# Macaron block with a mixture of experts: the two experts of a token found by MAX8 and FIND_INDEX8 instructions instead of pairwise comparison

## What is computed

```python
logits = xf @ gate_w                                  # (tokens, 8)
top_logits, top_idx = jax.lax.top_k(logits, 2)
top_gates = jax.nn.softmax(top_logits, axis=-1)
gates = jnp.sum(jax.nn.one_hot(top_idx, 8) * top_gates[..., None], axis=1)
h = gelu(jnp.einsum('nd,edh->neh', xf, w1) + b1)      # 8 experts, hidden 256
out_e = jnp.einsum('neh,ehd->ned', h, w2) + b2
routed = jnp.einsum('ne,ned->nd', gates, out_e)
shared = gelu(xf @ shared_w1 + shared_b1) @ shared_w2 + shared_b2
x = x + 0.5 * (routed + shared)
```

## The kernel before

| group | rank begins | TensorE stages after logits, with their plan start | place ready | place begins |
|---|---|---|---|---|
| 0 | 65.2 | hidden 65.1, acc 68.8 | 70.1 | 73.2 |
| 1 | 343.6 | hidden 342.9, hidden 346.7 | 348.5 | 350.4 |
| 2 | 780.5 | hidden 779.1, hidden 782.9 | 785.4 | 786.6 |
| 3 | 1141.0 | hidden 1140.9, hidden 1144.7 | 1145.9 | 1148.4 |

## Time and profile before

### The profile page before, as it was taken

How to read it: one execution, slowest core, us unless ns; L and a number is a source line. 1 busy time by engine, 2 the same in 40 slices (tenths; PEclk the granted TensorE clock), 3 DMA queues, 4 the chain that set the end, 5 groups by cost and what they waited for, 6 DMA issues and landing times.

```text
span 1339.3 us, 10709 instructions
## 1 busy us (share of the span) xinstructions
PE 1047.6 (78%) x3296; PEld 574.9 (43%) x3296; DVE 731.5 (55%) x1130; ACT 593.6 (44%) x1008; POOL 439.6 (33%) x429
## 2 busy tenths in 40 slices
PE   5998888982978878968938287867977698969884
PEld 3545555332534444444313142344444443536552
DVE  3311000067879898979999885978988520200000
ACT  3423433233425888557323333357666541314332
POOL 4153443202553353331000246032452212154442
PEclk8998999995989989979968587989988899779887
DMA  8954554424144675773344624265685425034544
GB/s 284 332 171 87 94 95 79 79 58 134 36 98 109 173 143 117 160 196 93 94 111 87 206 56 93 60 179 112 134 215 108 68 37 112 32 64 95 94 85 56
DMA packets 60204, 155.15 MB, mean 116 GB/s; under 512 B 10578, under 2 KB 10578, under 8 KB 57974
## 3 DMA queue, kind: packets, MB, share of 16 engines
q0 software_dynamic: 29568, 60.90, 26.9%
q1 hardware_dynamic: 30582, 93.58, 22.6%
HBM read 99.74 MB, written 58.88 MB: 118 GB/s over the span
## 4 chain that ended last, share of the span: by engine, by line
DMA 33%; PE 27%; DVE 12%; POOL 10%; ACT 8%; issue 8%; SPq 1%; POOLq 0%; ACTq 0%; DVEq 0%
DMA x_rows<-ys,into_i 14%; DMA out_rows<-ys,into_i 10%; PE misc L867 6%; POOL slots L1538 6%; PE hps L736 5%; DMA xs<-x_normal,rows_i 4%; PE yps L805 3%; PE hps L789 3%; PE yps L748 2%; PE xps L719 2%; DVE run L1355 2%; ACT ys L975 2%; DMA xin<-in_x 1%; DMA xin<-x_rows 1%; ACT xin L996 1%
## 5 line engine op out<-in xcount | busy, mean ns | idle before, releaser
L805 PE MATMUL yps<-w_all,hidden_sb 128*128 x368 | 209.5, 700 | 55.8 <-ACT hidden_sb L962 55.0
L789 PE MATMUL hps<-w_all,hidden_sb 128*128 x736 | 188.2, 403 | 8.5 <-ACT hidden_sb L945 8.5
L1355 DVE TENSOR_TENSOR_SCAN run<-pwx,trig 128x512 f32<-128x512 f32 x128 | 149.5, 1210 | 46.0 <-ACT trig L1046 45.2
L789 PEld LDWEIGHTS hps<-w_all,hidden_sb 128*128 128x128 f32 x736 | 148.3, 207 | 54.3 <-issue 36.3
L1550 POOL DMA_INDIRECT xs<-x_normal,rows_i x92 | 106.1, 1153 | 139.2 <-PE xps L780 119.9
L975 ACT ACTIVATE ys<-yps,slots 128x512 f32<-128x512 f32 x92 | 63.1, 686 | 169.8 <-PE yps L805 62.3
L1563 POOL DMA_INDIRECT out_rows<-ys,into_i x46 | 77.5, 1685 | 166.5 <-ACT ys L975 94.2
L805 PEld LDWEIGHTS yps<-w_all,hidden_sb 128*128 128x128 f32 x368 | 74.3, 214 | 131.8 <-issue 129.8
L736 PE MATMUL hps<-xnT,sw_sb 128*128 128x512 f32 x256 | 129.9, 662 | 0.8 <-ACT xnT L919 0.8
L1563 POOL DMA_INDIRECT x_rows<-ys,into_i x46 | 77.8, 1691 | 153.9 <-DMA x_rows<-ys,into_i 85.0
L748 PE MATMUL yps<-sw_sb,hidden_sb 128*128 128x512 f32 x256 | 124.0, 629 | 0.0
(11 more groups left out here) (199 smaller groups left out, 1587.4 us busy)
## 6 DMA issues: line engine op xcount, KB each, us to landing
qx<-q_cols SPq DMA_DIRECT2D x128, 256.0 KB
x_normal<-xin SPq DMA_DIRECT2D x32, 256.0 KB
w_all<-in_w_experts SPq DMA_DIRECT2D x8, 1024.0 KB, 8.3
xin<-x_rows SPq DMA_DIRECT2D x32, 256.0 KB, 4.7
turns_sb<-in_w_out SPq DMA_DIRECT2D x3, 1536.0 KB
xin<-in_x SPq DMA_DIRECT2D x16, 256.0 KB, 3.8
x_rows<-ys POOLq DMA_DIRECT2D x16, 256.0 KB
q_cols<-xin SPq DMA_DIRECT2D x16, 256.0 KB
```

Source lines behind the costliest of these rows:

```text
L789: t = PE.matmul(hps[:, bank, 0:H], xT[:, j % 2, c, :], w_all[:, bass.ds(expert[j] + c * H, H)], start=c == 0, stop=c == KC - 1)
L805: t = PE.matmul(yps[:, bank, :], hb[:, j % 2, ec, :], w_all[:, bass.ds(expert[j] + (KC * H + ec * D), D)], start=ec == 0, stop=ec == EC - 1)
L1355: t = VE.tensor_tensor_scan(run[:, c, :], pwx[:, n // M, :], trig[:, n % 2, c, :], 0.0, ALU.mult, ALU.add)
```

## The change

`rank_logits` is rewritten. Four `max` instructions, one for each tile of 128 tokens, read eight logits from PSUM and write them sorted (`most`), four `max_index` instructions read them again with the sorted values and write their places (`most_at`, uint32). `diff` is the difference of the first two sorted values; `sel` is a comparison of the first two places with the constants 0 to 7 (`expert_no`, a new iota on POOL in place of the two memsets of `two`); `chosen` is the sum of the two halves of `sel`. `lg`, `rank`, `lr` and `two` are gone. `chosen` is now the last of the five signalled steps (item 4), `diff` is item 2, and the PSUM bank of the logits is free after the last `max_index` (item 1). The planner's cost of `rank` goes from 4.8 to 3.0.

```diff
-            piece("DVE", ("rank", q), 4.8, ("PE", ("logits", q)), ...)
+            piece("DVE", ("rank", q), 3.0, ("PE", ("logits", q)), ...)
...
             elif s[0] == "logits":
-                xps_uses.append((s, ranking.at((s[1], 0))))
+                xps_uses.append((s, ranking.at((s[1], 1))))
...
-                pe.wait_ge(*ranking.at((GB * g + 1, 6)))
+                pe.wait_ge(*ranking.at((GB * g + 1, 4)))
...
-                act.wait_ge(*ranking.at((q, 10)))
+                act.wait_ge(*ranking.at((q, 2)))
...
-                VE.tensor_copy(lg[:, :, :], xps[:, bank, 0:TB * E].rearrange("p (t e) -> p t e", e=E)
-                               ).then_inc(*ranking.of((q, 0)))
+                for tb in range(TB):
+                    t = VE.max(most[:, tb, :], xps[:, bank, tb * E:(tb + 1) * E])
+                t.then_inc(*ranking.of((q, 0)))
                 vec.wait_ge(*ranking.at((q, 0)))
-                VE.tensor_tensor(cmp_b[:, :, :, :], other, own, ALU.is_equal).then_inc(*ranking.of((q, 1)))
-                VE.tensor_tensor(cmp_a[:, :, :, :], other, own, ALU.is_gt).then_inc(*ranking.of((q, 2)))
+                for tb in range(TB):
+                    t = VE.max_index(most_at[:, tb, :], most[:, tb, :], xps[:, bank, tb * E:(tb + 1) * E])
+                t.then_inc(*ranking.of((q, 1)))
+                if q > 0:
+                    vec.wait_ge(*gate_exp.at(q - 1))
+                VE.tensor_tensor(diff[:, :], most[:, :, 1], most[:, :, 0], ALU.subtract).then_inc(*ranking.of((q, 2)))
                 vec.wait_ge(*ranking.at((q, 1)))
-                VE.tensor_tensor(cmp_b[:, :, :, :], cmp_b[:, :, :, :], low, ALU.mult).then_inc(*ranking.of((q, 3)))
+                VE.tensor_tensor(sel[:, ts, :, :], most_at[:, :, 0:2, None].broadcast_to([P, TB, 2, E]),
+                                 expert_no[:, None, None, :].broadcast_to([P, TB, 2, E]),
+                                 ALU.is_equal).then_inc(*ranking.of((q, 3)))
                 vec.wait_ge(*ranking.at((q, 3)))
...
-                VE.tensor_scalar(chosen[:, ts, :], rank[:, :, :], 1.5, None, ALU.is_lt).then_inc(*ranking.of((q, 6)))
...
+                VE.tensor_tensor(chosen[:, ts, :], sel[:, ts, 0, :], sel[:, ts, 1, :],
+                                 ALU.add).then_inc(*ranking.of((q, 4)))
```

More of the change, by code:

```diff
@@ L150, in macaron @@
         block_of = sb("block_of", [P, NB])
-        two = sb("two", [P, 2])
         minus_half = sb("minus_half", [P, TB])
@@ L161, in macaron @@
         rstd_a = sb("rstd_attn", [P, 3, TB])
-        lg = sb("lg", [P, TB, E])
+        most = sb("most", [P, TB, E])
+        most_at = sb("most_at", [P, TB, E], mybir.dt.uint32)
+        expert_no = sb("expert_no", [P, E])
         cmp_a = sb("cmp_a", [P, TB, E, E])
         cmp_b = sb("cmp_b", [P, TB, E, E])
-        rank = sb("rank", [P, TB, E])
         sel = sb("sel", [P, GT, 2, E])
@@ L169, in macaron @@
         pair = sb("pair", [P, GT, 2, E])
-        lr = sb("lr", [P, TB, 2])
         diff = sb("diff", [P, TB])
@@ L310, in plan_job @@
             piece("PE", ("logits", q), 6.0, *kept_rows, *start[:1], bank=[("xps", ("DVE", ("rank", q)))])
-            piece("DVE", ("rank", q), 4.8, ("PE", ("logits", q)), *start[2:], *([("DVE", ("gates", q - 1))] if q else []),
+            piece("DVE", ("rank", q), 3.0, ("PE", ("logits", q)), *start[2:], *([("DVE", ("gates", q - 1))] if q else []),
                   *([("DVE", ("place", g - 1))] if g and not second else []))
@@ L586, in macaron @@
         stats_made = signal("s_stats", [(q, i) for q in staged("load", "DVE") for i in range(2)])
-        ranking = signal("s_ranking", [(q, i) for q in staged("rank", "DVE") for i in range(11)])
+        ranking = signal("s_ranking", [(q, i) for q in staged("rank", "DVE") for i in range(5)])
         gating = signal("s_gating", [(q, i) for q in staged("gates", "DVE") for i in (0, 1, 2, 7, 3, 4, 5, 6)])
@@ L1120, in rank_logits @@
                 ts = slice(q % GB * TB, (q % GB + 1) * TB)
-                other = lg[:, :, None, :].broadcast_to([P, TB, E, E])
-                own = lg[:, :, :, None].broadcast_to([P, TB, E, E])
-                low = before[:, None, :, :].broadcast_to([P, TB, E, E])
                 vec.wait_ge(*consts.at(16))
                 vec.wait_ge(*logits_made.at(q))
-                VE.tensor_copy(lg[:, :, :], xps[:, bank, 0:TB * E].rearrange("p (t e) -> p t e", e=E)
-                               ).then_inc(*ranking.of((q, 0)))
+                for tb in range(TB):
+                    t = VE.max(most[:, tb, :], xps[:, bank, tb * E:(tb + 1) * E])
@@ L1133, in rank_logits @@
                 vec.wait_ge(*ranking.at((q, 3)))
-                VE.tensor_tensor(cmp_a[:, :, :, :], cmp_a[:, :, :, :], cmp_b[:, :, :, :],
-                                 ALU.add).then_inc(*ranking.of((q, 4)))
-                vec.wait_ge(*ranking.at((q, 4)))
-                VE.tensor_reduce(rank[:, :, :], cmp_a[:, :, :, :], AX.X, ALU.add).then_inc(*ranking.of((q, 5)))
-                vec.wait_ge(*ranking.at((q, 5)))
                 if q >= GB:
                     vec.wait_ge(*counted.at(q // GB - 1))
-                VE.tensor_scalar(chosen[:, ts, :], rank[:, :, :], 1.5, None, ALU.is_lt).then_inc(*ranking.of((q, 6)))
@@ L1142, in rank_logits @@
-                VE.tensor_tensor(sel[:, ts, :, :], rank[:, :, None, :].broadcast_to([P, TB, 2, E]),
-                                 two[:, None, :, None].broadcast_to([P, TB, 2, E]),
-                                 ALU.is_equal).then_inc(*ranking.of((q, 7)))
-                vec.wait_ge(*ranking.at((q, 7)))
-                VE.tensor_tensor(pair[:, 0:TB, :, :], sel[:, ts, :, :], lg[:, :, None, :].broadcast_to([P, TB, 2, E]),
-                                 ALU.mult).then_inc(*ranking.of((q, 8)))
@@ L1148, in rank_logits @@
-                vec.wait_ge(*ranking.at((q, 8)))
-                VE.tensor_reduce(lr[:, :, :], pair[:, 0:TB, :, :], AX.X, ALU.add).then_inc(*ranking.of((q, 9)))
-                vec.wait_ge(*ranking.at((q, 9)))
-                if q > 0:
-                    vec.wait_ge(*gate_exp.at(q - 1))
-                VE.tensor_tensor(diff[:, :], lr[:, :, 1], lr[:, :, 0], ALU.subtract).then_inc(*ranking.of((q, 10)))
+                VE.tensor_tensor(chosen[:, ts, :], sel[:, ts, 0, :], sel[:, ts, 1, :],
+                                 ALU.add).then_inc(*ranking.of((q, 4)))
@@ L1587, in tables @@
                 GE.memset(gcols[:, :, 2 * (E + 1):BR], 0.0)
-                GE.memset(two[:, 0:1], 0.0)
-                GE.memset(two[:, 1:2], 1.0)
                 GE.memset(no_rows[:, :, 1], 0.0)
@@ L1594, in tables @@
                 GE.iota(steps_of[:, :], pattern=[[P, E]], base=0, channel_multiplier=0,
+                        allow_small_or_imprecise_dtypes=True)
+                GE.iota(expert_no[:, :], pattern=[[1, E]], base=0, channel_multiplier=0,
                         allow_small_or_imprecise_dtypes=True)
```

## The result

| | before | after |
|---|---|---|
| median | 1333.6 us of four runs (1325.69 to 1348.18) | 1299.18 us of four runs (1298.54 to 1300.38) |
| span of the profiled execution | 1339.3 us | 1297.3 us |
| TensorE, VectorE, ScalarE, POOL busy | 1047.6, 731.5, 593.6, 439.6 us | 1018.4, 718.9, 586.2, 447.5 us |
| mean granted TensorE clock | 0.878 | 0.894 |

The ratio on record is 0.9714, with a 95% interval of 0.9674 to 0.9755, so the kernel is some 38 us faster.

A forecast was written before the change was run, and what follows sets the result against it. No single engine was taken to bound the kernel. Group 3's 3.4 us passed whole and half of the others' 10.8 us made 8.8 us off the profiled 1340.6 us; against the median, 1330 us, range 1314 to 1350.

The forecast's parts named there:

- The new ranking, 1.8 us: Each rank on VectorE: 1.8 us against 3.28, with 12 instructions for the sorted values and their places.
- The bank, nothing: Logits' PSUM bank is free 1.3 us after the rank begins, before at 0.2; costed at nothing, at worst 1.1 us.
- Job 4's rank, 1.5 us: In the attention stretches, where VectorE is nearly full, job 4's shorter rank gives 1.5 us.
- Group 3, 3.4 us whole: At the kernel's end the counting comes before the second `hidden` stage: 3.4 us less, passed on whole.
- Group 0, 1.9 of 3.9 us: Counting moves ahead of `acc`, 3.9 us earlier; the first block also waits for TensorE, so only 1.9 us gained.
- Group 1, a toss, 3.4 us: Counting ready exactly when the second `hidden` is; taken as moved ahead of it, 3.4 us less, a coin's toss.
- Group 2, 4.0 us: Counting stays, but `gates` goes before the gelu and VectorE's `place`, so the scatter begins 4.0 us earlier.
- The rival of an order that falls well: Shared-expert stages leave the way of the last attention batch's rows: 1318 us, with like luck before it 1310; chance 0.1.
- The two rivals by order: TensorE's order near the last attention batch turns against the kernel, 1350 us, chance 0.2, or falls well, 1310 us, chance 0.1.

The follow-up runs named there:

- the hand-made swap: New ranking, planner's cost 4.8, group 3's counting and job 7's exponential moved ahead of job 7's hidden and gelu; against the kernel before: 1335.36 us, 0.9993.
- the one that I tried: Attention sines moved ahead of block copies in ScalarE's order; ratios to the kernel before: 1.0054 in that kernel, 0.9989 in the new ranking with cost 1.6.

## Why the prediction was wrong

**The new ranking, 1.8 us.** Right, and a little dear: 1.57 us. The four MAX8 took 0.39 us together, a pitch of 0.08; the pairs came every 0.14 us, as two instructions, by the larger count that was taken. At a lone instruction's price for each it would have been 2.8 us; that didn't hold, for no wait stands inside the two fours and their instructions overlap in the rows: the FIND_INDEX8 that starts at 55.61 lasts to 55.78, and the next MATCH_VALUE_LOAD starts at 55.69. (The Trainium skill, "VectorE: DVE Perf Modes", section "The TRN2 errata", which the prediction set beside this end, speaks of instructions that read SBUF. MAX8 and FIND_INDEX8 read PSUM here, so these rows don't test it on them.) (That finding the index is a pair is as the Trainium skill, "VectorE: DVE Perf Modes", section "Two Vector instructions with no wait between them", lists it; the trace agrees, with 0.07 and 0.17 us for the two.)

**The bank, nothing.** No run contradicts it: new instructions with 4.8 leave the time at 0.9997.

**Job 4's rank, 1.5 us.** Not seen. New instructions with 4.8 leave the time unchanged within 5 us, and the 3.8 us by which VectorE was less busy between the scans came back as idle time there. "Nearly full" is not "bounding": before, it was idle 114.7 of 757 us, and waits can take up what a shorter rank gives.

**Group 3, 3.4 us whole.** Right at its place: from the end of the logits to the first scatter issue 14.4 us before, 1124.02 - 1113.99 = 10.0 after, 4.4 less; the hand-made swap gave 3.1. Whether it reached the end whole, the swap's 0.9993 (0.9957 to 1.003) can't tell.

**Group 0, 1.9 of 3.9 us.** The counting did move. The logits of job 1 end at 55.07 and the first scatter issue is at 65.14: 10.1 us, where before it was 73.96 - 59.83 = 14.1, so 4.0 less. But the reason for passing on only half failed. TensorE in order of time, of after:

```profile
54.92 5.38 PE L736 MATMUL hps<-xnT,sw_sb 128*128 128x512 f32 x8
60.14 0.34 PE L757 MATMUL xps<-chosen,earlier 128*128 128x72 f32 x2
...
97.33 0.60 PE L780 MATMUL xps<-ident,xs 128*128 128x128 f32 x4
97.77 3.64 PE L719 MATMUL xps<-gate_sb,xnT 128*128 128x8 f32 x32
```

The first block's `x` now stands ahead of the logits of job 2, behind which the earlier trace rows had it. The forecast took over the old order of that place. The first add came 10.9 us earlier (109.14 against 120.05): 4.0 from the counting, 2.1 from what lies behind it, and 4.8 because the logits had ended earlier to begin with, of which more below. The number for jobs 0 to 2 alone measured 0.9931, 9 us less (4 to 14), where the forecast had 1.9 us, halved: this term was too small.

**Group 1, a toss, 3.4 us.** The toss was won and brought nothing at its place. The counting came behind one `hidden`, yet VectorE did `gates` behind `place`, where before it came ahead of it, so that the scatter waited for `told`: 15.4 us from the logits' end to the first issue, where before it was 13.2. The number for job 3 alone, with 15.2 us there, still measured 0.9966 (0.9934 to 0.9998), between nothing and 9 us, by other moves than the one forecast.

**Group 2, 4.0 us.** Wrong. `gates` was to come ahead of `place`. VectorE and ScalarE in order of time, of after:

```profile
776.47 0.20 DVE L1185 TENSOR_TENSOR cmp_a<-xps,steps_of 128x64 f32<-128x64 f32 x1
...
782.40 0.17 DVE L1155 TENSOR_SCALAR told<-gr 128x8 f32<-128x8 f32 x1
...
783.29 0.68 DVE L1366 TENSOR_TENSOR outT<-trig 128x512 f32<-128x512 f32 x1
```

```profile
771.01 0.61 ACT L1043 ACTIVATE trig<-trig 128x512 f32<-128x512 f32 x1
...
774.20 1.28 ACT L926 ACT_TABLE_LOAD   x1
775.49 0.21 ACT L926 ACTIVATE gr<-diff 128x4 f32<-128x4 f32 x1
```

The new order put sines of the attention ahead of the exponential, which in the old one came behind it (the exponential at 784.92, the first of these sines at 785.04). `place` came first, and the scatter, at 783.39, came 19.6 us after the logits of job 5 had ended at 763.8, 2 us more than before. The earlier part of the new plan isn't to blame: with the number for job 5 alone nothing moves before it, and the sines come first all the same. Played through, the shorter rank lets VectorE make the input of the next attention step's sines at 784.8, so they are ready for ScalarE when `a_norm` ends at 785.2, together with the exponential, and have the longer way to the end. The forecast asked which of the stages that it knew there would pass which, and not what else a shorter rank makes ready.

**What failed.** The moves forecast for groups 3 and 0 came, with 4.4 and 4.0 us at their places; those for groups 1 and 2 did not gain there. What failed is the step under the sum, that only the neighbours of the rank move, so that four places make up the whole effect. The order is a list made by one play-through. Between the two kernels' lists 230 of TensorE's 584 positions, 264 of ScalarE's 633, 118 of VectorE's 359 and 75 of POOL's 249 differ. For the 755.8 us between the scans, which gave 22.6 us, the forecast had counted 1.5 us for job 4, 3.4 for group 1 and 4.0 for group 2, halved, and none of the three came at its place. The rival of an order that falls well had this mechanism, at a chance of 0.1, and was sized from three stages of one place and its like (12 and 20 us below the forecast); the kernel came out 31 below. Its own chances don't quite fit together either: 0.09 for less than 1312 us is nearly the whole 0.1 of a rival whose two sizes were 1318 and 1310. The two rivals by order shared 0.3 of the chance, with sizes taken from one short stretch of 37 us. The trace of before had 114.7 us of VectorE's idle time between the scans to gain from, and that row was to be had. The planner's own end would not have warned of it: it moves by 9.1, about the size of the forecast.

**What stays open.** That the order does it is shown, by the old ranking with 3.0; how much of that goes by way of the higher granted clock isn't (some 12 of the 38 us come together with it). That more than half of it is the stretch of batches 2 and 3 beside the blocks of group 2 is shown by the stretches and by job 5. Which moves in it do it isn't: the one that I tried made it worse. Nor can it be asked engine by engine: with the new list for TensorE, ScalarE or VectorE alone and the old ones for the others, the engines would wait for each other in a ring. Nor is it shown that the new order is good; of the kernels that differ only in numbers none was measurably slower than before, so it may be that the old order was an unlucky one.

## What to carry to other kernels

Where program order comes out of a list scheduler, a cost constant is part of the code: time the instruction edit and the constant apart, since the constant alone was worth 3% here and the instructions nothing that could be told. Don't follow a new constant through the neighbours of its stage with the plan times of the old play; bound what a new order can gain in a stretch by the idle time of the fullest engine there (114.7 us here, of which 17.7 went), and ask of a shorter stage what else it makes ready. What an order can lose isn't bounded so. Two or three other values of such a constant are cheap experiments; keep the order that is measured fastest, for the planner's own end misjudged 38 us as 9 and had the sign wrong for two kernels.

## What the chip showed beyond that

The same opening ran at different speeds. The kernel with 3.0 for jobs 4 and 5 has, in the opening, TensorE's order of the kernel before, instruction by instruction. TensorE in order of time, of before and of that kernel:

```profile
17.95 6.19 PE L736 MATMUL hps<-xnT,sw_sb 128*128 128x512 f32 x8 [0.77 <-ACT xnT L919]
23.98 4.58 PE L719 MATMUL xps<-gate_sb,xnT 128*128 128x8 f32 x32
28.41 12.96 PE L736 MATMUL hps<-xnT,sw_sb 128*128 128x512 f32 x24
```

```profile
17.61 3.67 PE L736 MATMUL hps<-xnT,sw_sb 128*128 128x512 f32 x8 [0.77 <-ACT xnT L919]
21.11 3.63 PE L719 MATMUL xps<-gate_sb,xnT 128*128 128x8 f32 x32
24.60 10.55 PE L736 MATMUL hps<-xnT,sw_sb 128*128 128x512 f32 x24
```

And tables of stretches, the first two of before, the third of that kernel (the clock is the third number from the end):

```profile
14.00:26.00 12.00, 10.68 (x39) 6.41 (x38) 2.81 (x6) 5.89 (x8) 5.72 (x15) 1.00 0.69 211
26.00:33.00 7.00, 7.00 (x21) 4.42 (x21) 4.57 (x26) 1.66 (x3) 2.74 (x8) 0.53 1.03 353
```

```profile
15.00:30.00 15.00, 14.23 (x61) 9.19 (x62) 7.82 (x45) 7.99 (x11) 7.01 (x19) 1.00 0.89 298
```

Two things slow the opening of before. From 26 to 33 us the granted clock is 0.53 of full speed, near the lower of its two levels, though TensorE had been busy without a gap from 17.95 us on; the other kernel has 1.00 there. And the first eight matmuls of a kind last 6.19 us instead of 3.67, the first five of them 1.06 us each by median instead of 0.59, while the column says 1.00. The changed kernel has 1.00 from 15 to 30 us too, and its first eight are slow as well:

```profile
16.83 5.99 PE L736 MATMUL hps<-xnT,sw_sb 128*128 128x512 f32 x8 [0.77 <-ACT xnT L919]
```

So the column doesn't tell the speed of these first matmuls. The logits of job 1 ended at 59.83 us in before, at 53.60 in the kernel with jobs 4 and 5, and at 55.07 in the changed one; over the ten kernels with that opening they ended between 52.7 and 59.8 us. So some 5 of the 11.6 us of the opening, between the two traces, needn't be the change, and such differences between executions of one order may be part of the 22 us that the runs of before span. The medians don't rest on one such execution. What decides the speed there no run shows.
